# Half of the masked value copies of an attention moved from VectorE to ScalarE

## What is computed

```
qkv = x @ Wqkv.T + b                      # 12 heads of 16 features
att = softmax(einsum("bhid,bhjd->bhij", q, k) * 16**-0.5)
out = einsum("bhij,bhjd->bhid", att, v)   # 16 tokens per image, so 16 x 16 per head
h = h + out @ Wout.T + bout
```

## Time and profile before

| | |
|---|---|
| median of 3 runs | 491.46 us (491.12 to 492.39) |
| profiled execution | 496.69 us, its span 494.8 us, mean granted clock 0.81 |
| TensorE busy | 400.9 us, 81% |
| VectorE busy | 391.2 us, 79% |
| ScalarE busy | 228.1 us, 46% |
| GpSimd busy | 121.9 us, 25% |
| chain that ended last | TensorE 42%, VectorE 38%, ScalarE 8% |
| L1102, all 80 copies | 37.3 us, mean 537 ns |

### The profile page before, as it was taken

The page is one execution under the profiler, slowest core; times in us unless marked ns, Lnnn a source line. Parts: engine busy times, 40 slices in busy tenths (PEclk is TensorE's granted clock), DMA queues, the critical chain, the costliest instruction groups (busy, mean ns, idle before and its releaser), DMA issues.

```text
span 494.8 us, 9007 instructions
## 1 busy us (share of the span) xinstructions
PE 400.9 (81%) x3570; PEld 283.6 (57%) x3570; DVE 391.2 (79%) x883; ACT 228.1 (46%) x391; POOL 121.9 (25%) x182
## 2 busy tenths in 40 slices
PE   4677857989777989999992998696799178798976
PEld 4676727769663667766761443234368036656965
DVE  3899999589887845498787679988899859777974
ACT  4477373644836668845511296010293022362261
POOL 3525344042242225233313026602202020000000
PEclk9968885596757989999986899896699578588686
DMA  8545000004014000200000000000000000000000
GB/s 279 222 121 231 2 2 1 1 1 146 1 29 191 2 1 1 95 2 1 1 0 2 1 0 0 0 1 1 1 1 1 1 1 1 1 1 2 11 24 33
DMA packets 4237, 17.53 MB, mean 35 GB/s; under 512 B 858, under 2 KB 1763, under 8 KB 3683
## 3 DMA queue, kind: packets, MB, share of 16 engines
q1 hardware_dynamic: 4194, 16.95, 9.4%
HBM read 16.16 MB, written 0.79 MB: 34 GB/s over the span
## 4 chain that ended last, share of the span: by engine, by line
PE 42%; DVE 38%; ACT 8%; issue 6%; POOL 4%; DMA 1%; SPq 0%; DVEq 0%; ACTq 0%; POOLq 0%
PE PS L1523 36%; DVE R L1102 4%; POOL rstd L522 3%; PE PS L1655 2%; DVE R L1374 2%; DVE R L1376 2%; DVE R L995 2%; PE PS L1662 2%; DVE R L1427 1%; DMA T<-tok_w 1%; DVE Q L1092 1%; DVE stats L1005 1%; DVE stats L958 1%; POOL ve L519 1%; DVE xn L1015 1%
## 5 line engine op out<-in xcount | busy, mean ns | idle before, releaser
L1523 PE MATMUL PS<-Q,R 128*128 128x32 f16 (+3 forms) x1024 | 46.1, 191 | 13.7 <-DVE R L1102 10.2
L1523 PE MATMUL PS<-m,Q 128*128 128x192 f16 (+1 forms) x576 | 52.8, 247 | 2.4 <-DVE Q L1318 2.4
L1523 PEld LDWEIGHTS PS<-Q,R 64*64 64x64 f16 (+1 forms) x1024 | 44.2, 125 | 16.9 <-DVE R L1102 10.7
L1523 PEld LDWEIGHTS PS<-m,Q 128*128 128x128 f16 (+1 forms) x576 | 46.5, 97 | 11.6 <-issue 7.8
L519 POOL TENSOR_SCALAR ve<-mv 128x1 f32<-128x1 f32 x56 | 14.5, 259 | 148.1 <-DVE mv L1006 128.9
L1523 PE MATMUL PS<-X_hi,R 128*128 128x512 f16 x144 | 42.2, 399 | 0.0
L1318 DVE TENSOR_TENSOR Q<-Q 128x512 f16<-128x512 f32 x36 | 26.1, 739 | 19.6 <-ACT Q L805 19.6
L1523 PE MATMUL PS<-R,K 128*128 128x512 f32 x66 | 35.0, 653 | 6.4 <-DVE R L1416 6.4
L1523 PE MATMUL PS<-X_hi,late_a 128*128 128x512 f16 (+1 forms) x72 | 31.4, 460 | 10.2 <-DVE X_hi L1082 5.6
L800 ACT ACTIVATE Q<-PS,col 128x512 f32<-128x512 f32 x36 | 24.8, 689 | 31.5 <-PE PS L1523 31.5
L1102 DVE TENSOR_SCALAR R<-Q,K 128x1024 f16<-128x1024 f16 x80 | 37.3, 537 | 0.3
(11 more groups left out here) (231 smaller groups left out, 934.2 us busy)
## 6 DMA issues: line engine op xcount, KB each, us to landing
R<-tok_x SPq DMA_DIRECT2D x8, 480.0 KB, 3.6
T<-tok_w SPq DMA_DIRECT2D x6, 480.0 KB, 7.7
T<-late SPq DMA_DIRECT2D x1, 2632.0 KB, 8.7
T<-moe SPq DMA_DIRECT2D x1, 2304.0 KB, 8.5
T<-moe SPq DMA_DIRECT2D x1, 1728.0 KB, 8.0
T<-full SPq DMA_DIRECT2D x1, 1152.0 KB, 4.9
R<-early SPq DMA_DIRECT2D x1, 776.0 KB, 10.3
out<-H SPq DMA_DIRECT2D x4, 192.0 KB, 1.9
```

Of the source, the lines that this page charges most:

```text
L1523: return T_.matmul(o, w, x, start=start, stop=stop, skip_group_check=True)
```

## The change

In each half VectorE makes the copies for heads 0 to 3 of VA only, and ScalarE makes those for heads 4 to 7, as Copy activations with the mask column as scale, at the start of its step `st`, before that step's weight pieces. They wait for the low part of VA (`qkv_ready` at 5n + 3) and for TensorE's last transposes of the former half, and count a new semaphore, `bd_act`. TensorE's `values` waits for `bd_act` in addition.

```diff
+        bd_act = sem("bd_act")
...
+                def spread(hf):
+                    act.wait_ge(qkv_ready, 5 * (2 * a + hf) + 3)
+                    if 2 * a + hf:
+                        filled(("vb", a, hf - 1, 1, 1) if hf else ("vb", a - 1, 1, 1, 1))
+                    v = VAbd.rearrange("p l s (h j) -> p l s h j", h=HA)
+                    w = pairs["VA"].rearrange("p l (s j) -> p l s j", j=SEQ)
+                    for h in range(HA // 2, HA):
+                        ins = nc.scalar.activation(v[:, :, :, h], w, ACT.Copy, scale=K[:, K_HM + h:K_HM + h + 1])
+                    ins.then_inc(bd_act, 1)
+
                 for step, hf in ATTENTION_ORDER:
                     if (step, hf) in before:
                         before[step, hf]()
+                    if step == "st":
+                        spread(hf)
...
-                    for h in range(nh):
+                    for h in range(HA // 2 if src == "VA" else nh):
                         ins = V.tensor_scalar(v[:, :, :, h], w, K[:, mask + h:mask + h + 1], None, ALU.mult)
...
                     pe.wait_ge(bd_ready, 3 * (2 * a + hf) + 3)
+                    pe.wait_ge(bd_act, 2 * a + hf + 1)
```

## The result

| | before | after |
|---|---|---|
| median | 491.92 us (491.12 to 492.48) | 499.99 us (499.65 to 501.26) |
| profiled execution, span | 496.69, 494.8 us | 499.65, 497.8 us |
| mean granted clock | 0.810 | 0.822 |
| TensorE busy | 400.9 us | 396.1 us |
| VectorE busy | 391.2 us | 381.4 us |

The change makes the kernel slower: ratio 1.017, 95% interval 1.0145 to 1.0195, 8.1 us where 7.0 were forecast; the time lies in the range. (491.92 us is the median of four executions of before, 491.46 us that of the three known ahead of the prediction.) VectorE gave up 9.8 us of work and ScalarE took 16.2 us. The profiled execution of before took some 5 us more than the median, at a mean clock of 0.810 where a second trace of the same program, further down, has 0.843.

A forecast was written before the change was run, and what follows sets the result against it. The engine late at each half's `values0` was taken to decide, above all ScalarE behind a DMA in the first attention's second half. Stall 5.25 - gain 1.0 + clock 2.75 = +7.0 us on 491.46: 498.5 us, range 495.2 to 501.0.

The forecast's parts named there:

- Relief of VectorE buys nothing: All four halves: taking four copies off VectorE in each, 6.5 us of its time in all, directly gains zero.
- Price of a copy: ScalarE, every half: one copy takes 1.11 us alone, four take 4.2 us; bounds 3.7 to 6.0 us for four.
- First half: First attention: value copies stay covered; later weight pieces keep GpSimd off the fourth KVB copy, gaining 1.0 us (bounds 0, 1.0).
- Second half: First attention: ScalarE's copies follow a weight piece waiting for a DMA, so TensorE starts `values0` 5.25 us later.
- The clock: Second half of first attention: after the idle time TensorE's clock is low from `values0` to softmax, costing 2.75 us (bounds 0, 2.75).
- Third and fourth half: Second attention: ScalarE's copies end at 419.3 and 465.7, before TensorE's `values0` at 422.53 and 467.80; cost zero.
- D: Second half of first attention: the transfer lands early, no stall, only the 1.0 us gain remains: 490.5 us; chance 0.05.
- C: Every half: copies are slower on ScalarE and each half pays 0.9 us, +3.6 us, 495.1 us; chance 0.03.
- A: Second half of first attention: the clock costs nothing, not falling or low there anyway; +4.25 us, 495.7 us; chance 0.17.
- E: Whole kernel: smaller stall offset by the gain, no change that can be told, within 1.5 us; chance 0.05.

The follow-up runs named there:

- the kernel with low parts later: Kernel before, no copies on ScalarE, its four weight pieces of step st 0 held until VectorE has made the KVB copies: 491.2 us, ratio 1.0007.
- the partner: Kernel before, unchanged, traced and timed a second time: 490.8 us, ratio 0.9979, span 488.2 us.
- the moved piece: The change, with one ScalarE weight piece moved so the second half's copies precede the piece waiting for the load: 490.4 us, 0.9975 of before.
- the two stall kernels: Kernel before, no ScalarE copies; TensorE waits before `values0` of the first attention's second half for the third or fifth weight piece after the load: 497.2, 500.6 us.

## Why the prediction was right

Direction, place and size came out: 499.99 us against 498.5, range 495.2 to 501.0. By its own steps:

- *Relief of VectorE buys nothing.* Right in the second attention (0.9992). In the first half it was right as told, that TensorE doesn't wait for the value copies, but too simple: without the relief the later low parts would have met them (2.10 us of waiting in the kernel with low parts later).
- *Price of a copy.* 1.11 us predicted, 1.136 measured; four in 4.2 and 4.25 us. "ScalarE: Activation LUTs", in the Trainium skill, rules for kernel authors, gives VectorE up to about a factor of three per element in bf16; here, in f16 and with 0.41 us there, it is 2.8. It speaks of the price of a copy, which didn't decide: the same sixteen copies cost nothing in another order.
- *First half.* Gain of 1.0 us: 7.96 to 6.94 us of waiting, and GpSimd's pause as described. The Trainium skill's page "SBUF — State Buffer", "Who interferes with whom", says that VectorE in its two-port modes and GpSimd exclude each other and that ScalarE never waits. The trace agrees: VectorE's copies are slow beside low parts, while ScalarE's four copies took 4.26 us here, where GpSimd made low parts until 73.37, and 4.25 us at 463.86, where it made none.
- *Second half.* The mechanism is the one predicted, down to the order on ScalarE. The stall was mis-sized: 5.25 us predicted, 3.89 of idle time measured. The step took TensorE's arrival and the load's from one execution in which TensorE came 0.2 us behind the load's arrival (119.76 and 119.57); in the second trace of before it is 0.8 us, and in after it is 1.6 us (114.59 and 112.97), the outputs of the first half having run at 1.2 GHz nearly throughout. The lag gained up to `values0` is 5.0 us all the same, by 4.1 us at the stall and 0.9 us ahead of it that the prediction doesn't have.
- *The clock.* "After 5.25 us without work I expect it low, 2.75 us more." In after it was low before the stall began and rose at 122.5, in the midst of the transposes; in the partner too it was low when `values0` began and rose at 116.4, and from there to VectorE's first softmax instruction it takes 4.4 us, not the 3.75 of the first trace (5.6 in after). So the clock cost 1.15 us there (3.6 to 4.7 in the table), not 2.75. What was not foreseen is the second place, 3.3 us at the start of the experts. The two terms that were too high (1.4 us for the stall, 1.6 for the clock) are nearly made up for by the one left out: 7.0 predicted, 8.1 measured against the runs of that comparison, 9.2 against the second series of before. That the size came out is luck to this extent.
- *Third and fourth half.* Covered, 2.2 and 2.3 us of slack left in after, 3.2 and 2.1 predicted.
- *The rivals.* D, the stall that isn't there, is what the moved piece makes of the change: 490.4 us, where 490.5 was worked out. C fell with the same run. A was refuted in its price by the two stall kernels, which cost more than their length; one of its grounds, that the clock is low at this spot in ordinary executions anyway, held in the partner, and the clock's price came for the most part elsewhere. E fell by the result.

## What to carry to other kernels

Ahead of moving work to an idle engine, read that engine's own queue at the point of insertion: an engine that is busy for half of the span can still be standing behind a transfer at the moment that counts, and everything placed after that wait inherits it. Put the new work ahead of the wait, not after it. When VectorE and GpSimd share a stretch, look at which of the copies meet which of GpSimd's instructions; a move is worth something if it keeps them apart, and it can be worth more than the work it saves.

## What the runs showed of the hardware

A stall of TensorE cost more than its length: 2.97 and 5.09 us of idle time made the kernel before 6.2 and 9.6 us slower, and 3.89 us in the change went with 8.1 us. In the change 3.3 us of it arise some 60 us later, at an idle time that both kernels have. In ten of the 14 traces the clock rose between 83 and 87 us of the first half, in four between 94 and 99 us; the two traces of before, of one program, are one of each kind. VectorE copies that take 0.41 us alone took 1.3 us on average in a stretch full of GpSimd's subtractions (eight in 10.37 us), while against twelve of VectorE's copies in a row a single subtraction of GpSimd took 6.04 us in place of 1.28. The latter in the trace of after:

```profile
99.12 6.04 POOL L528 TENSOR_TENSOR R<-T,R 128x576 f16<-128x576 f32 x1 [16.84 <-ACT T L705]
114.30 1.28 POOL L528 TENSOR_TENSOR m<-T,m 128x576 f16<-128x576 f32 x1 [9.15 <-ACT T L705]
...
99.19 4.83 DVE L1115 TENSOR_SCALAR R<-Q,K 128x1024 f16<-128x1024 f16 x12
```
